# Identity products on TensorE in the first four chunks of a selective scan

## The chip, the core and the metric

The kernel runs on one core of one Trainium2 chip. The metric is the device time of one execution in microseconds (us). In what follows PE is TensorE, DVE is VectorE, ACT is ScalarE, POOL is GpSimd and SP is the engine that issues most transfers.

## What is computed

The input is 2 sequences of 1024 tokens with 256 features. Four blocks follow one another, each with a residual sum and a layer norm ahead of it: a selective state-space scan, a mixture of 8 experts (top 2, with a capacity), linear attention with 16 heads, and a gated feed-forward layer. The scan is the part that matters here:

```python
A = -jnp.exp(A_log)                                  # 256 features x 64 states
def step(h, inp):
    dt, b, xt, c = inp
    dA = jnp.exp(dt[:, :, None] * A)
    h = dA * h + dt[:, :, None] * b[:, None, :] * xt[:, :, None]
    y = jnp.einsum('bdn,bn->bd', h, c)
    return (h, y)
```

Each of the 2 x 1024 tokens thus updates a state of 256 x 64 numbers and reads it out once.

## The kernel before

`prepare` norms and projects the tokens and writes the factors of the scan to HBM as sums of bf16 parts. `selective_scan` then goes over 32 chunks of 64 tokens (16 chunks a sequence), and each chunk over 8 groups of 16 pairs of features. There are 256 groups, numbered gi; c = gi // 8 is the chunk and j = gi % 8 the group in it. `rest` does the experts, the attention and the feed-forward layer.

For a group the engines do this, in the names and lines of the profile:

- PE computes the exponents of the decays into two PSUM banks, `bank_a` (L911, 16 products of 64 columns in bf16, function `decays`). There is one pair of these banks, so `decays(gi)` waits until ACT has read those of the group before (semaphore `exp`, L904).
- ACT turns them into decays (L1045, two exponentials a group) and, in all chunks but the first of a sequence, puts the carried state of the chunk before into the input (L1055, `hand_on`), which POOL has computed (L1315, L1321). In ACT's order the hand-on of group gi stands behind both exponentials of group gi + 1.
- PE computes the inputs of the recurrence (L930, 16 products in bf16) into one of two double banks, `bank_in`. It waits there for the scan two groups back (L925).
- DVE runs the recurrence over the group (L1160, one instruction of 128 x 1024).
- From group 10 on, PE reads the states of the chunk before out (L944, function `y`), four float32 products of 32 rows by 512 columns at a time, behind the inputs of every even group.

`scan_schedule` writes one list, and every engine goes through it in this order. PE's `stream(gi)` issues `decays(gi + 1)` and then the inputs of group gi. The first product on a new chunk's tokens is L970, which waits for the transfer of the chunk (`tokens_ld`). From group 34 on, every odd group is preceded by `stay_awake`: two bf16 products of 128 x 512 on a constant matrix (L898), written over a bank that `decays` fills directly afterwards. Nobody reads their result. The constant, `tri`, is loaded and cast only at group 32. Ahead of that PE has no such products.

A float32 product stands as two records in the profile, a float32 transpose as one.

Of the kernel before, what the change touches and what calls it, by code (L numbers as in the profile page):

```python
# [7 lines left out]
P = 128  # L8
# [46 lines left out]
class Kit:  # L55
# [11 lines left out]
    def sem(self, name):  # L67
        if name not in self.named:
            self.named[name] = self.ctx.enter_context(self.nc.semaphore("s_" + name))
        return self.named[name]  # L70
# [47 lines left out]
CPB = SEQ // T  # L118
G = 16
GROUPS = P // G  # L120
# [660 lines left out]
def selective_scan(k, a, s):  # L781
    pe, act, dve, pool, sp, sem = k.pe, k.act, k.dve, k.pool, k.sp, k.sem
    ident, eps, slots = s["ident"], s["eps"], s["slots"]
    with ExitStack() as ctx:
# [28 lines left out]
        bank_a = [k.banks[0], k.banks[1]]  # L813
# [79 lines left out]
        def on_pe():  # L893
            def stay_awake(bank):

                pe.wait_ge(sem("tri"), 1)
                for _ in range(2):
                    pe.q.matmul(bank, tri[:, 1, :], tri[:, 1, :].unsqueeze(1).broadcast_to([P, 4, P]), start=True, stop=True)  # L898

            def decays(gi):  # L900
                c, j = divmod(gi, GROUPS)
                pe.wait_ge(sem(f"rows_ld{c % 2}"), ROWS_LD * (c // 2 + 1))
                if gi:
                    pe.wait_ge(sem("exp"), 2 * gi)  # L904
                if j % 2 and gi > GROUPS * CPB // 4 + 1:
                    stay_awake(bank_a[1])
                for i in range(8):
                    for half in range(2):
                        g, q = divmod(first_d(j, half) + i, RCH)
                        strip = slice(32 * g, 32 * (g + 1))  # L910
                        ins = pe.q.matmul(bank_a[half][:, i * T:(i + 1) * T], s["astat"][strip, RCH * g + q, :],  # L911
                                          rows[strip, c % 2, q, :], start=True, stop=True)
                ins.then_inc(sem("prod"), 1)

            def stream(gi):
                c, j = divmod(gi, GROUPS)
                if gi == 0:
                    pe.wait_ge(sem("astat_ld"), 16 * ROWG * DH * 3)
                    wait_prepared(k, pe)
                    decays(0)  # L920
                if gi + 1 < TOTAL:
                    decays(gi + 1)
                pe.wait_ge(sem(f"tokens_ld{c % 2}"), TOKENS_LD * (c // 2 + 1))
                if gi >= 2:
                    pe.wait_ge(sem("scan"), gi - 1)  # L925
                for half in range(2):
                    d = slice(first_d(j, half), first_d(j, half) + 8)
                    for b in range(BLKS):
                        to = per_d(bank_in[gi % 2])[:, 8 * half:8 * half + 8, S * b:S * (b + 1)]
                        ins = pe.q.matmul(to.rearrange("p d (s e) -> p s d e", e=2), bstat[0:ROWS, c % 2, b, :],  # L930
                                          xdiag[0:ROWS, c % 2, b, :, d, :], start=True, stop=True)
                ins.then_inc(sem("inputs"), 1)
# [27 lines left out]
            for kind, *x in schedule:  # L960
# [59 lines left out]
                elif kind == "rank":  # L1020
# [9 lines left out]
                    for i in range(n - 1):  # L1030
# [3 lines left out]
                                start=False, stop=True).then_inc(sem("r_rank"), 1)  # L1034
# [308 lines left out]
        on_sp()  # L1343
        on_act()
        on_pe()
        on_dve()
        on_pool()
# [655 lines left out]
```

## Time and profile before

| | |
|---|---|
| three timed executions | 1318.41, 1318.73, 1331.76 us; median 1318.73 |
| profiled execution | 1323.35 us, span 1321.8 us |
| mean granted TensorE clock | 0.913 |
| PE busy | 1116.7 us, 84% of the span |
| DVE busy | 842.4 us, 64% |
| ACT busy | 502.7 us, 38% |
| DVE, the recurrence (L1160) | 256 instructions, 565.3 us busy, from 100.9 to 694 us of the span |
| PE, read-out (L944) | 1024 records, 155.0 us |
| PE, `stay_awake` (L898) | 222 records, 69.0 us |

The span falls into `prepare` (to about 96 us), the scan (to about 694 us), the routing and scatter of the last tokens (to 738 us), the experts (to about 1025 us), and attention and feed-forward. The clock column of the profile gives the mean granted clock of a stretch as a share of 2.4 GHz: 0.50 is 1.2 GHz throughout, 1.00 is 2.4 GHz throughout.

### The profile page before, as it was taken

The numbers are of one execution on the slowest core, as the hardware profiler recorded it, in microseconds if no ns is written. First come the engines' busy times: TensorE is split into PE (matmuls) and PEld (weight loads), VectorE is DVE, ScalarE is ACT, GpSimd is POOL, SyncE is SP. The second block draws the span as 40 slices with busy tenths as digits, with TensorE's granted clock in tenths as the row PEclk, the third lists the DMA queues.
The fourth block names the chain that finished last, engine by engine and source line by source line (L and its number), as shares of the span: only waits on it lengthen the run. The fifth ranks groups of instructions, "written<-read, shape, count | busy, mean of one in ns | idle before, by whom it ended". The sixth has DMA issues, their size and how long they took to land.

```text
span 1321.8 us, 29499 instructions
## 1 busy us (share of the span) xinstructions
PE 1116.7 (84%) x11952; PEld 705.4 (53%) x11952; DVE 842.4 (64%) x1006; ACT 502.7 (38%) x1245; POOL 306.9 (23%) x930
## 2 busy tenths in 40 slices
PE   3637888889888888889884799999999488999998
PEld 2425444445444454444442578888887244475565
DVE  5858999999999999999993111121111577742211
ACT  2865555566655665566551111111111110122110
POOL 9741222222233222522242011111111100000000
PEclk8765789989999898998996799999999798999999
DMA  3797345543222222322223822222200400000000
GB/s 106 235 283 217 76 99 128 132 115 84 55 64 70 56 60 48 85 57 50 52 70 143 299 95 102 100 100 99 79 17 12 131 0 0 0 9 8 16 16 16
DMA packets 171687, 112.02 MB, mean 85 GB/s; under 512 B 93637, under 2 KB 162248, under 8 KB 169248
## 3 DMA queue, kind: packets, MB, share of 16 engines
q1 hardware_dynamic: 163120, 88.69, 24.2%
q0 software_dynamic: 8000, 20.87, 4.8%
q8 instruction: 94, 1.54, 0.5%
q10 hardware_dynamic: 432, 0.59, 0.2%
q14 instruction: 41, 0.34, 0.1%
HBM read 63.18 MB, written 45.90 MB: 83 GB/s over the span
## 4 chain that ended last, share of the span: by engine, by line
PE 48%; DVE 27%; issue 13%; ACT 4%; DMA 3%; SPq 2%; POOL 1%; DVEq 0%; POOLq 0%; ACTq 0%
DVE h L1160 19%; PE psum L1410 11%; PE psum L1422 10%; PE psum L1894 8%; PE psum L1905 4%; PE psum L944 3%; DVE den L1724 2%; PE psum L1850 2%; PE psum L930 2%; ACT decay L1045 2%; PE psum L911 2%; DMA b_parts_d<-b_parts 1%; PE psum L1842 1%; PE psum L1881 1%; PE psum L898 1%
## 5 line engine op out<-in xcount | busy, mean ns | idle before, releaser
L1160 DVE TENSOR_TENSOR_SCAN h<-decay,psum 128x1024 f32<-128x1024 f32 x256 | 565.3, 2266 | 16.9 <-ACT psum L1055 9.9
L1045 ACT ACTIVATE decay<-psum 128x512 f32<-128x512 f32 x512 | 279.3, 600 | 201.9 <-PE psum L911 197.1
L930 PE MATMUL psum<-xdiag,bstat 96*128 96x64 bf16 x4096 | 178.5, 201 | 50.2 <-DVE h L1160 47.2
L930 PEld LDWEIGHTS psum<-xdiag,bstat 96*128 96x128 bf16 x4096 | 146.8, 102 | 76.4 <-DVE h L1160 68.1
L911 PEld LDWEIGHTS psum<-rows,shared 32*128 32x128 bf16 x4096 | 79.8, 97 | 186.9 <-issue 120.3
L944 PE MATMUL psum<-h,cstat 128*32 128x512 f32 x1024 | 155.0, 683 | 1.6 <-DVE h L1160 1.6
L1410 PE MATMUL psum<-xdt,shared 128*128 128x320 f32 x512 | 141.7, 438 | 0.7 <-ACT xdt L1469 0.7
L1422 PE MATMUL psum<-shared,hid 128*128 128x256 f32 x640 | 139.5, 379 | 0.6 <-ACT hid L1463 0.6
L1315 POOL TENSOR_TENSOR carry<-decay,h 128x16 f32<-128x16 f32 x240 | 57.9, 241 | 343.9 <-ACT decay L1045 343.6
L1422 PEld LDWEIGHTS psum<-shared,hid 128*128 128x128 f32 x640 | 121.0, 190 | 17.2 <-issue 1.1
L911 PE MATMUL psum<-rows,shared 32*128 32x64 bf16 x4096 | 111.4, 196 | 15.4 <-ACT decay L1045 7.5
L1410 PEld LDWEIGHTS psum<-xdt,shared 128*128 128x128 f32 x512 | 98.7, 193 | 41.7 <-issue 2.8
L1894 PE MATMUL psum<-xt,wgu 128*128 128x512 f32 x256 | 112.8, 600 | 2.5 <-DVE at L1729 2.5
L1497 DVE TENSOR_SCALAR hid<-psum 128x320 f32<-128x320 f32 x64 | 31.4, 491 | 112.9 <-PE psum L1410 112.9
L1532 POOL DMA_INDIRECT picked_d<-eo,to x40 | 39.0, 975 | 259.5 <-ACT eo L1466 134.2
L898 PE MATMUL psum<-r_tri 128*128 128x512 bf16 x222 | 69.0, 393 | 28.8 <-ACT decay L1045 28.2
L1500 DVE TENSOR_SCALAR eo<-psum,gate 128x256 f32<-128x256 f32 x20 | 9.7, 484 | 116.9 <-PE psum L1422 111.2
L1894 PEld LDWEIGHTS psum<-xt,wgu 128*128 128x128 f32 x256 | 49.1, 192 | 64.2 <-issue 59.4
L1747 DVE TENSOR_TENSOR shared<-psum,sil 128x512 f32<-128x512 f32 x32 | 22.0, 691 | 81.5 <-PE psum L1894 81.5
L1463 ACT ACTIVATE hid<-psum 128x320 f32<-128x320 f32 x64 | 28.0, 437 | 119.1 <-PE psum L1410 119.1
L1818 ACT ACTIVATE sil<-psum 128x512 f32<-128x512 f32 x32 | 19.1, 597 | 131.2 <-PE psum L1894 127.1
L1321 POOL TENSOR_TENSOR carry<-carry,u 128x16 f32<-128x16 f32 x240 | 52.9, 221 | 24.0 <-ACT u L1083 3.6
(194 smaller groups left out, 1103.0 us busy)
## 6 DMA issues: line engine op xcount, KB each, us to landing
shared<-in_w SPq DMA_DIRECT2D x16, 1024.0 KB, 4.8
xdiag<-x_parts_d SPq DMA_DIRECT2D x256, 48.0 KB
x_parts_d<-x_parts POOLq DMA_DIRECT2D x46, 256.0 KB, 8.0
parts_d<-dt_parts SPq DMA_DIRECT2D x24, 256.0 KB, 8.5
rows<-parts_d SPq DMA_DIRECT2D x128, 48.0 KB
disp_d<-zero SPq DMA_DIRECT2D x4, 1305.0 KB, 8.5
xd<-disp_d SPq DMA_DIRECT2D x8, 652.5 KB, 6.3
picked_d<-zero SPq DMA_DIRECT2D x4, 1024.0 KB, 5.2
```

What stands on the lines that cost most here:

```text
L898: pe.q.matmul(bank, tri[:, 1, :], tri[:, 1, :].unsqueeze(1).broadcast_to([P, 4, P]), start=True, stop=True)
L911: ins = pe.q.matmul(bank_a[half][:, i * T:(i + 1) * T], s["astat"][strip, RCH * g + q, :], rows[strip, c % 2, q, :], start=True, stop=True)
L930: ins = pe.q.matmul(to.rearrange("p d (s e) -> p s d e", e=2), bstat[0:ROWS, c % 2, b, :], xdiag[0:ROWS, c % 2, b, :, d, :], start=True, s ...
L944: ins = pe.q.matmul(bank_y[32 * q:32 * q + 32, :].rearrange("p (s d e) -> p s d e", s=2, e=4), s["cstat"][:, tok // 4, :], h[:, first:last ...
L1045: act.q.activation(decay[:, gi % NB, 8 * half:8 * half + 8, :], per_d(bank_a[half]), ACT.Exp).then_inc(sem("exp"), 1)
L1160: dve.q.tensor_tensor_scan(out=h[:, half_slot(c, half), ch:ch + G, :].rearrange("p d t -> p (d t)"), data0=decay[:, gi % NB, :, :].rearran ...
L1315: pool.q.tensor_tensor(whole, first, h[:, half_slot(c - 1, half), ch:ch + G, T - 1], ALU.mult).then_inc(sem("carry_made"), 1)
L1321: pool.q.tensor_tensor(whole.rearrange("p (h i) -> p h i", h=2), whole.rearrange("p (h i) -> p h i", h=2), own, ALU.add).then_inc(sem("car ...
L1410: ins = pe.q.matmul(table.bank(key)[:, 0:half_cap], w1[:, e % 2, dh, f * P:(f + 1) * P], xdt[:, e % 2, dh, c * half_cap:(c + 1) * half_cap ...
L1422: ins = pe.q.matmul(table.bank(key)[:, 0:D], hid[:, e % 2, f, st * P:(st + 1) * P], w2[:, e % 2, f, :], start=f == 0, stop=f == FT - 1)
L1894: ins = pe.q.matmul(table.bank(key)[:, :], wgu[:, j, dh, f * P:(f + 1) * P], xt[:, u, dh, :], start=dh == 0, stop=dh == 1)
L1905: ins = pe.q.matmul(table.bank(key)[:, 0:D], gt[:, blk % 2, f, n * P:(n + 1) * P], wd[:, f, :], start=f == 0, stop=f == FT - 1)
```

## The change

A second helper, `wake`, issues one float32 product of the identity with itself over 256 columns, into the first half of the second bank of `bank_a`. `decays` calls it behind its wait for `exp` and ahead of its own products: for the groups 1 to 10 all, and for the odd groups from 11 to 33. These are 22 products. `ident` is there from the start of `prepare`. The result is overwritten by `decays` and is read by nobody. No wait is added, and nothing else of the program changes.

```diff
--- before.py
+++ after.py
@@ -897,11 +897,17 @@
                 for _ in range(2):
                     pe.q.matmul(bank, tri[:, 1, :], tri[:, 1, :].unsqueeze(1).broadcast_to([P, 4, P]), start=True, stop=True)
 
+            def wake(bank):
+
+                pe.q.matmul(bank[:, 0:2 * P], ident[:, :], ident[:, :].unsqueeze(1).broadcast_to([P, 2, P]), start=True, stop=True)
+
             def decays(gi):
                 c, j = divmod(gi, GROUPS)
                 pe.wait_ge(sem(f"rows_ld{c % 2}"), ROWS_LD * (c // 2 + 1))
                 if gi:
                     pe.wait_ge(sem("exp"), 2 * gi)
+                if gi and (j % 2 or gi <= GROUPS + 2) and gi <= GROUPS * CPB // 4 + 1:
+                    wake(bank_a[1])
                 if j % 2 and gi > GROUPS * CPB // 4 + 1:
                     stay_awake(bank_a[1])
                 for i in range(8):
```

Lines behind the helper move down by 6, so that L911 is L917 in the changed kernel, and so on. The new product is L902.

On PE, at the start of the scan, this stood before (L609 is the last of `prepare`; the two first groups' exponents follow it):

```order
L609 MATMUL psum<-ident,sp_r 128x128 x8
L911 MATMUL psum<-rows,shared 128x64 x32
L930 MATMUL psum<-xdiag,bstat 128x4x8x2 x16
L911 MATMUL psum<-rows,shared 128x64 x16
L930 MATMUL psum<-xdiag,bstat 128x4x8x2 x16
```

and this stands there now:

```order
L609 MATMUL psum<-ident,sp_r 128x128 x8
L917 MATMUL psum<-rows,shared 128x64 x16
L902 MATMUL psum<-ident 128x256
L917 MATMUL psum<-rows,shared 128x64 x16
L936 MATMUL psum<-xdiag,bstat 128x4x8x2 x16
L902 MATMUL psum<-ident 128x256
L917 MATMUL psum<-rows,shared 128x64 x16
L936 MATMUL psum<-xdiag,bstat 128x4x8x2 x16
```

The second group's exponents, and with them the first group's inputs, now stand behind an identity product.

On PE, where the second chunk begins, this stood before (L970 is the product that waits for the chunk's tokens, L944 the first read-out):

```order
L930 MATMUL psum<-xdiag,bstat 128x4x8x2 x16
L970 MATMUL psum<-xdiag,bstat 128x128
L911 MATMUL psum<-rows,shared 128x64 x16
L930 MATMUL psum<-xdiag,bstat 128x4x8x2 x16
L911 MATMUL psum<-rows,shared 128x64 x16
L930 MATMUL psum<-xdiag,bstat 128x4x8x2 x16
L911 MATMUL psum<-rows,shared 128x64 x16
L930 MATMUL psum<-xdiag,bstat 128x4x8x2 x16
L944 MATMUL psum<-h,cstat 32x512 x4
```

and this stands there now:

```order
L976 MATMUL psum<-xdiag,bstat 128x128
L902 MATMUL psum<-ident 128x256
L917 MATMUL psum<-rows,shared 128x64 x16
L936 MATMUL psum<-xdiag,bstat 128x4x8x2 x16
L902 MATMUL psum<-ident 128x256
L917 MATMUL psum<-rows,shared 128x64 x16
L936 MATMUL psum<-xdiag,bstat 128x4x8x2 x16
L902 MATMUL psum<-ident 128x256
L917 MATMUL psum<-rows,shared 128x64 x16
L936 MATMUL psum<-xdiag,bstat 128x4x8x2 x16
L950 MATMUL psum<-h,cstat 32x512 x4
```

The exponents of the chunk's second and third groups stand behind an identity product too; from there on only each second group's do, and these are the groups whose `decays` is followed by a read-out.

## Rows read from the trace of the kernel before

**Rows 1.** The page: granted clock in 40 slices of 33 us, in tenths.

```profile
PEclk8765789989999898998996799999999798999999
```

**Rows 2.** What DVE's recurrence waited for: us in total, times.

```profile
  ACT psum L1055: 9.9, 17
  POOL decay L1324: 5.5, 1
```

**Rows 3.** Timeline of DVE: start, us, instruction, count, in brackets the idle time ahead.

```profile
100.87 17.53 DVE L1160 TENSOR_TENSOR_SCAN h<-decay,psum 128x1024 f32<-128x1024 f32 x8 [5.47 <-POOL decay L1324]
119.70 6.64 DVE L1160 TENSOR_TENSOR_SCAN h<-decay,psum 128x1024 f32<-128x1024 f32 x3 [1.30 <-ACT psum L1055]
126.82 4.46 DVE L1160 TENSOR_TENSOR_SCAN h<-decay,psum 128x1024 f32<-128x1024 f32 x2 [0.48 <-ACT psum L1055]
131.98 4.46 DVE L1160 TENSOR_TENSOR_SCAN h<-decay,psum 128x1024 f32<-128x1024 f32 x2 [0.70 <-ACT psum L1055]
137.06 13.25 DVE L1160 TENSOR_TENSOR_SCAN h<-decay,psum 128x1024 f32<-128x1024 f32 x6 [0.61 <-ACT psum L1055]
150.83 8.82 DVE L1160 TENSOR_TENSOR_SCAN h<-decay,psum 128x1024 f32<-128x1024 f32 x4 [0.52 <-ACT psum L1055]
159.87 17.53 DVE L1160 TENSOR_TENSOR_SCAN h<-decay,psum 128x1024 f32<-128x1024 f32 x8 [0.23 <-ACT psum L1055]
178.20 2.29 DVE L1160 TENSOR_TENSOR_SCAN h<-decay,psum 128x1024 f32<-128x1024 f32 x1 [0.80 <-ACT psum L1055]
```

**Rows 4.** Busy time by stretch: PE, PEld, DVE, ACT, POOL, then clock, DMA share, GB/s.

```profile
98.00:115.00 17.00, 12.50 (x256) 10.61 (x256) 14.13 (x7) 9.12 (x18) 1.72 (x10) 0.50 0.84 247
118.00:135.00 17.00, 16.02 (x244) 9.62 (x238) 14.53 (x8) 9.53 (x30) 4.43 (x23) 0.50 0.75 198
135.00:142.00 7.00, 5.23 (x140) 3.51 (x137) 6.39 (x4) 5.14 (x16) 1.76 (x9) 0.96 0.47 80
180.00:190.00 10.00, 8.36 (x186) 4.48 (x179) 10.00 (x7) 5.42 (x16) 2.93 (x15) 1.00 0.56 160
```

**Rows 5.** Timeline of PE: two groups of chunk 0, and a read-out at half clock.

```profile
98.81 0.61 PE L911 MATMUL psum<-rows,shared 32*128 32x64 bf16 x16 [2.54 <-ACT decay L1045]
100.59 0.61 PE L911 MATMUL psum<-rows,shared 32*128 32x64 bf16 x16 [0.21 <-ACT decay L1045]
...
128.17 1.94 PE L944 MATMUL psum<-h,cstat 128*32 128x512 f32 x8
130.04 0.60 PE L911 MATMUL psum<-rows,shared 32*128 32x64 bf16 x16
```

**Rows 6.** Timeline of PE: the nearest products, at full clock and at half.

```profile
182.09 0.60 PE L898 MATMUL psum<-r_tri 128*128 128x512 bf16 x2 [0.61 <-ACT decay L1045]
182.62 0.41 PE L911 MATMUL psum<-rows,shared 32*128 32x64 bf16 x16
...
508.54 2.05 PE L955 MATMUL psum<-w_out,y_t 128*128 128x256 f32 x4
510.38 0.88 PE L898 MATMUL psum<-r_tri 128*128 128x512 bf16 x2
```

**Rows 7.** Timeline of all engines where the second chunk begins.

```profile
117.65 0.28 PE L970 MATMUL psum<-xdiag,bstat 12*128 12x128 bf16 x1 [2.50 <-DMA xdiag<-x_parts_d]
```

**Rows 8.** Timeline of PE in `prepare`.

```profile
35.51 1.09 PE L569 MATMUL psum<-ident,xa 128*128 128x128 f32 x4 [4.30 <-DVE xa L477]
39.34 1.40 PE L609 MATMUL psum<-ident,sp_r 128*128 128x128 f32 x8 [0.18 <-DVE sp_r L514]
40.58 1.88 PE L579 MATMUL psum<-xn_t,w_proj 128*128 128x512 f32 x4
```

**Rows 9.** Busy time by stretch around them, columns as in Rows 4.

```profile
36.00:38.00 2.00, 2.00 (x11) 2.00 (x10) 1.20 (x1) 1.43 (x2) 2.00 (x5) 0.50 0.21 14
40.00:42.00 2.00, 2.00 (x11) 1.28 (x10) 2.00 (x4) 1.64 (x3) 0.66 (x2) 1.00 0.10 30
```

**Rows 10.** Waits of DVE from 186 to 700 us: total, times, longest.

```profile
DVE h L1160 <- ACT psum L1055: 5.3, 10, 1.0
DVE h L1160 <- PE psum L930: 1.1, 2, 0.9
```

## The prediction, made before the changed kernel ran

> **What bounds the kernel now.** The change touches the scan's first 34 groups alone, so I ask which engine sets the pace there. I began with the page's clock line [rows 1]: the third to sixth slices, which hold the end of `prepare` and the first chunks of the scan, show 6, 5, 7 and 8 tenths, and only then does the clock stay near full. Next I asked what DVE's recurrence waited for [rows 2], because 256 instructions of 2.2 us each fill most of the 594 us of the scan: it waited 9.9 us for the hand-on of the carried state and 5.5 us for its very first group. DVE is thus the bound, and the change can win only time in which DVE stood idle. The timeline gives each gap [rows 3]. Chunk 0 runs without one, 8 recurrences in 17.53 us (2.19 us each). Chunk 1 begins 1.30 us late. Then come six gaps, 0.48 + 0.70 + 0.61 + 0.52 + 0.23 + 0.80 = 3.34 us. The recurrences of the groups behind 178.20 us are outside the change.
>
> The six gaps are PE's. From 118 to 135 us PE was busy for 16.02 of 17 us at clock 0.50, which is 1.2 GHz [rows 4], and two recurrences that DVE does in 4.46 us came every 131.98 - 126.82 = 5.16 us [rows 3]. At that clock a read-out takes 130.04 - 128.17 = 1.87 us [rows 5]. Where the clock is at its upper level, 2.4 GHz, and two `stay_awake` products stand ahead of every second group, PE has room: 8.36 us busy of 10 and DVE busy throughout [rows 4]. In that kernel part the products stand in the same place in each pair of groups as the new ones will.
>
> The gap of 1.30 us is not PE's clock but a transfer: L970 sat 2.50 us and started at 117.65 us when the chunk's tokens landed [rows 7]. DVE had ended chunk 0 at 118.40 us (100.87 + 17.53) and began chunk 1 at 119.70 us [rows 3], 2.05 us behind L970.
>
> **The cost of one identity product.** The trace has none. It is bounded from two sides by the nearest rows [rows 6]. Two bf16 products over 512 columns took 182.62 - 182.09 = 0.53 us at 2.4 GHz. Two float32 products over 256 columns took 510.38 - 508.54 = 1.84 us at 1.2 GHz, 0.92 us each, half of which is 0.46 us at 2.4 GHz. A float32 product over 256 columns is what is added, so it costs 0.5 us at 2.4 GHz and 0.95 us at 1.2 GHz; the bounds are 0.46 to 0.53 and 0.92 to 1.06 us. It stands behind PE's wait for ACT and ahead of `decays`, so it lengthens the loop in which `decays` waits for ACT's exponentials and ACT waits for `decays`.
>
> **Chunk 0, a loss.** The clock is 0.50 when the scan begins [rows 4]. The first recurrence waits for the inputs of group 0, which now stand behind one identity product: +0.95 us. The loop took 100.59 - 98.81 = 1.78 us a group [rows 5], hidden under DVE's 2.19 us. With the product it takes 2.73 us while the clock is low: the second recurrence is late by about 0.1 us (the first was ready half a microsecond early), each further one by 2.73 - 2.19 = 0.54 us. At 2.4 GHz the loop is below 1.78 + 0.5 - 0.2 us (0.61 us of `decays` shrinks to 0.41 [rows 5, 6]), some 2.1 us, and hidden. How soon the clock rises is not shown. It rose within 40.6 - 35.5 = 5 us of the start of nearly gapless full-size products in `prepare` [rows 8, 9]; chunk 0 had small products only, 12.50 us busy of 17, and it did not rise at all [rows 4]. So the ends are 5 us, two groups, and the whole chunk, eight. Full-size products now fill 0.95 of 2.73 us, so it will be later than 5 us; I take four groups, of which the recurrence pays 0.1 + 0.54, and part of one more: 0.8 us. Chunk 0 ends 0.95 + 0.8 = 1.75 us later, at 120.15 us. The ends are +1.05 and 0.95 + 0.1 + 6 x 0.54 = +4.3 us.
>
> **The step into chunk 1.** DVE had 1.30 us to spare here, and the transfer lands when it did. Behind L970 one more identity product stands ahead of the second group's exponents, and the hand-on of the first group stands behind these on ACT: 2.05 + 0.5 - 0.2 = 2.35 us behind 117.65 us is 120.0 us at 2.4 GHz, and 2.05 + 0.95 = 3.0 us, 120.65 us, at 1.2 GHz. DVE begins at the later of this and its own end of chunk 0, near 120.15 us: 0.45 us later than before. The ends are +0.3 us and 118.40 + 4.3 - 119.70 = +3.0 us.
>
> **The six gaps, a gain.** If the clock is at its upper level from there on, PE's work in a pair of groups is that of 180 to 190 us, where DVE had no gap [rows 4]. All 3.34 us go. If the clock falls as often as before, none goes and each product adds to a pair that is full already. I take the first, since the same place in the order with the same PE time held the clock at 1.00 there.
>
> **The sum.** +0.45 - 3.34 = -2.9 us against the profiled execution's 1323.35 us: 1320.5 us. Nothing between chunk 4 and the end of the scan has slack ahead of DVE, so the shift reaches the end. The three timed executions have their median 4.6 us below the profiled one, so the time to forecast is 1318.73 - 2.9 = 1315.8, rounded to **1316 us**. Its own range is 1312 to 1320: the ends of the first two terms, and the later gaps. For these are not constant. After 186 us DVE still lost 5.3 + 1.1 us [rows 10] in places where the clock fell for some microseconds in spite of `stay_awake`; where they fall hangs on how the scan lies in time, and a shift of some microseconds may take or add 3 us.
>
> **Rival one: the clock rises late** (slower than before). The mechanism is the loop through ACT. In chunk 0 the identity products lengthen it past DVE's pace from the second group on. If the clock is still low when chunk 1 begins, the step costs +3.0 us, the products of groups 9 and 10 another 2 x 0.95 on a PE without room, and one more pair 0.95 us; after that the clock is up, and 0.61 + 0.52 + 0.23 + 0.80 = 2.16 us of gaps go. Net +3.0 + 1.9 + 0.95 - 2.16 = +3.7 us: 1322.4 us. It decides where chunk 0 has more than about seven groups at 1.2 GHz. For it speaks that from 118 to 135 us PE was all but gaplessly busy and the clock stayed low [rows 4]; against it, that these were narrow products and the new ones are full-size.
>
> **Rival two: identity products don't raise the clock.** Then the step costs +3.0, groups 9 and 10 cost 1.9, and the twelve odd groups 11 to 33 between 8 x 0.95 (those in stretches that were at 1.2 GHz) and 12 x 0.95: together +12.5 to +16.3 us, in the middle 1333 us. Against it stand rows of `prepare`: from 35.51 to 40.58 us PE ran nothing but products with the identity (L569, L609) [rows 8], and the clock went from 0.50 to 1.00 [rows 9]. The Trainium skill, page "TensorE: Matmul & The Clock Gate", section "Part 4: PE-mode transpose", says that the upper clock level does not engage for transposes. By that rule the products of `prepare` would not have raised it, and identity products here might be no better; the trace disagrees. The new product is moreover a plain product and no transpose.
>
> **Rival three: nothing is left of it.** The gain is made, and the later clock drops, shifted by 3 us, take it back: 1318.7 us, give or take 2. For it speaks that the later gaps sum to 6.4 us, twice the gain [rows 10].
>
> **How the numbers follow.** Forecast 0.55, late rise 0.2, no rise 0.05, nothing left 0.2. The range reaches from the forecast's lower end over rival three to just above rival one, 1312 to 1324.5 us; outside are rival two and the tails. One per cent is 13.2 us, about what a measurement of this kernel can tell from no change. DVE's idle time ahead of all recurrences together, 9.9 + 5.5 us and little more, would have to vanish for a gain of that size: 0.01. Slower by as much only by rival two and not all of it: 0.04. The rest, 0.95, is within 1%.
>
> **What would show it.** In the profile after: the first recurrence about 1 us later; the clock at 1.00 within chunk 0, by about 110 us, and through 118 to 178 us; DVE without gaps in chunks 1 to 3 and about 0.5 us late at group 8; the recurrence of group 33 some 3 us earlier than 178.2 us; L902 at 0.5 us. A clock of 0.50 in 120 to 135 us would prove the forecast wrong, as would gaps of 1 us or more between pairs of recurrences there; a scan that is 3 us shorter with a total that is not would speak for rival three.

## The result, and the profile after

The changed kernel took 1327.63 us in the median of 19 runs (1321.08 to 1334.23), the kernel before 1322.74 us in as many (1315.98 to 1331.76). The ratio is 1.0037, 95% interval 1.0019 to 1.0055: 0.37% slower, some 4.9 us, where 2.9 us faster was forecast. The profiled execution took 1331.37 us, its span is 1329.9 us. Of the ten timed runs of the second measurement of the changed kernel, one took 5321.5 us and is not in its ratio below.

The page of the changed kernel gives the granted clock in 40 slices of 33 us. It answers to [rows 1]: the fourth slice is still at 5 tenths, the fifth at 8.

```profile
PEclk9865899998998898998996799999999798999999
```

What the recurrence waited for (us in total, times), as in [rows 2]. A new entry stands first: the inputs of the recurrence themselves, PE's products, now come late. Of its 13.4 us, 8.22 lie ahead of the first recurrence; before, that wait was 5.5 us under another name [rows 2].

```profile
  PE psum L936: 13.4, 10
  ACT psum L1061: 12.2, 20
```

The timeline of DVE in the changed kernel (start, us, instruction, count, in brackets the idle time ahead) answers to [rows 3].

```profile
101.07 4.46 DVE L1166 TENSOR_TENSOR_SCAN h<-decay,psum 128x1024 f32<-128x1024 f32 x2 [8.22 <-PE psum L936]
106.14 2.29 DVE L1166 TENSOR_TENSOR_SCAN h<-decay,psum 128x1024 f32<-128x1024 f32 x1 [0.61 <-PE psum L936]
109.08 2.29 DVE L1166 TENSOR_TENSOR_SCAN h<-decay,psum 128x1024 f32<-128x1024 f32 x1 [0.65 <-PE psum L936]
...
120.90 2.29 DVE L1166 TENSOR_TENSOR_SCAN h<-decay,psum 128x1024 f32<-128x1024 f32 x1 [0.71 <-PE psum L936]
124.10 2.29 DVE L1166 TENSOR_TENSOR_SCAN h<-decay,psum 128x1024 f32<-128x1024 f32 x1 [0.92 <-ACT psum L1061]
...
139.67 2.29 DVE L1166 TENSOR_TENSOR_SCAN h<-decay,psum 128x1024 f32<-128x1024 f32 x1 [1.09 <-ACT psum L1061]
...
145.55 41.66 DVE L1166 TENSOR_TENSOR_SCAN h<-decay,psum 128x1024 f32<-128x1024 f32 x19 [0.66 <-ACT psum L1061]
187.13 0.40 DVE L1190 TENSOR_TENSOR x1o<-psum,xres 128x256 f32<-128x256 f32 x1
```

In chunk 0 a recurrence now starts every 2.94 us (109.08 - 106.14) and not every 2.19. From group 15 at 145.55 us to group 33 there is no gap at all. PE's timeline shows the loop, and the price of one product at either clock.

```profile
109.19 1.22 PE L902 MATMUL psum<-ident 128*128 128x256 f32 x2 [0.21 <-ACT decay L1051]
110.34 0.61 PE L917 MATMUL psum<-rows,shared 32*128 32x64 bf16 x16
110.88 1.03 PE L936 MATMUL psum<-xdiag,bstat 96*128 96x64 bf16 x16
112.13 1.22 PE L902 MATMUL psum<-ident 128*128 128x256 f32 x2 [0.21 <-ACT decay L1051]
...
121.01 1.22 PE L902 MATMUL psum<-ident 128*128 128x256 f32 x2
122.16 0.61 PE L917 MATMUL psum<-rows,shared 32*128 32x64 bf16 x16
...
145.40 0.70 PE L902 MATMUL psum<-ident 128*128 128x256 f32 x2 [0.45 <-ACT decay L1051]
146.03 0.41 PE L917 MATMUL psum<-rows,shared 32*128 32x64 bf16 x16
```

A product holds the exponents back by 110.34 - 109.19 = 1.15 us at 1.2 GHz and by 146.03 - 145.40 = 0.63 us at 2.4 GHz; the loop is 112.13 - 109.19 = 2.94 us. The stretches (PE, PEld, DVE, ACT, POOL, clock, DMA share, GB/s) show when the clock rose; they answer to [rows 4].

```profile
98.00:115.00 17.00, 14.51 (x188) 9.97 (x186) 11.36 (x6) 6.50 (x12) 0.63 (x5) 0.50 0.75 217
118.00:135.00 17.00, 16.27 (x198) 10.00 (x199) 12.98 (x6) 7.16 (x23) 3.04 (x16) 0.50 0.73 170
135.00:142.00 7.00, 6.78 (x89) 4.04 (x89) 5.22 (x3) 3.01 (x8) 1.17 (x6) 0.50 0.01 2
142.00:149.00 7.00, 6.47 (x120) 3.25 (x117) 5.74 (x3) 3.92 (x14) 1.76 (x9) 0.89 0.26 41
149.00:160.00 11.00, 8.90 (x186) 5.40 (x190) 11.00 (x6) 6.35 (x17) 2.93 (x15) 1.00 0.25 70
```

It did not rise in chunk 0 at all, and only in chunk 1: 0.89 over the 7 us from 142 us puts the rise at about 143.5 us, 8 us later than before (0.96 over the 7 us from 135 us [rows 4], 135.5 us). The times of rise and fall below are read in the same way.

To compare many kernels I cut each profile at five points of DVE's timeline: the first recurrence, the end of group 7, the start of group 8, the start of group 15, and the end of group 33 (the first residual sum). From group 33 to the end of the last recurrence no kernel here is changed. In us:

| kernel | chunk 0 | step | 8 to 15 | 15 to 33 | sum | 33 to end |
|---|---|---|---|---|---|---|
| before | 17.53 | 1.30 | 17.36 | 43.35 | 79.54 | 513.8 |
| before, second profile | 17.53 | 1.25 | 16.64 | 43.03 | 78.45 | 513.5 |
| the change | 22.12 | 0.91 | 21.45 | 41.58 | 86.06 | 515.0 |
| the change, second profile | 22.55 | 0.91 | 17.37 | 41.43 | 82.26 | 511.1 |
| groups 1 to 10 only | 22.55 | 0.91 | 16.83 | 42.97 | 83.26 | 512.0 |
| odd groups 11 to 33 only | 17.53 | 0.92 | 16.82 | 41.44 | 76.71 | 511.0 |
| the same, again | 17.53 | 0.45 | 16.65 | 41.43 | 76.06 | 513.3 |
| odd groups 17 to 33 only | 17.45 | 0 | 16.61 | 41.40 | 75.46 | 511.1 |
| odd 11 to 33, bf16 | 17.53 | 0.20 | 16.63 | 41.40 | 75.76 | 509.5 |
| burst only | 17.45 | 0 | 16.64 | 43.33 | 77.42 | 519.7 |
| burst and the change | 22.13 | 0.91 | 17.97 | 41.43 | 82.44 | 511.1 |
| longer burst and the change | 19.98 | 0.91 | 17.97 | 41.44 | 80.30 | 509.7 |
| four products in groups 1 to 4 | 23.10 | 0.91 | 17.97 | 41.44 | 83.42 | 513.8 |
| the change, bf16 | 20.85 | 0.72 | 17.60 | 41.39 | 80.56 | 520.4 |
| the change, half size | 19.13 | 0.49 | 18.33 | 41.40 | 79.35 | 508.8 |

Behind the scan all spans agree, 626.1 to 628.5 us. The step aside, the first four columns follow the edits for the most part. Where chunk 0 has no products, the step hangs on when the chunk's tokens land, and differs between two profiles of one program (0.92 and 0.45 us). The last column differs by up to 11.6 us between profiles though no edit touches it. Its two highest values are from single executions 8 and 10 us above the median of their kernel (1331.15 against 1323.31 us for the bf16 change, 1328.71 against 1319.18 us for the burst). So one total tells little of an edit worth 3 us.

### The profile page after: what moved, and what is told of

Read it like the earlier page. It is cut to its first block, busy times and chain, and to the rows that moved or that the text cites. A ratio compares the mean times of both kernels' runs of the same rounds, so it can differ in the third digit from the quotient of the medians.

```text
span 1329.9 us, 29587 instructions
## 1 busy us (share of the span) xinstructions
PE 1132.8 (85%) x11996; PEld 713.5 (54%) x11996; DVE 843.9 (63%) x1006; ACT 502.2 (38%) x1245; POOL 307.2 (23%) x930
## 4 chain that ended last, share of the span: by engine, by line
PE 48%; DVE 28%; issue 13%; ACT 4%; SPq 3%; DMA 2%; POOL 1%; DVEq 0%; ACTq 0%; POOLq 0%
DVE h L1166 20%; PE psum L1416 11%; PE psum L1428 10%; PE psum L1900 8%; PE psum L1911 4%; PE psum L950 3%; DVE den L1730 2%; PE psum L1856 2%; PE psum L936 2%; PE psum L917 2%; ACT decay L1051 2%; PE psum L902 1%; PE psum L1848 1%; PE psum L1887 1%; SPq L199 1%
## 5 line engine op out<-in xcount | busy, mean ns | idle before, releaser
L1166 DVE TENSOR_TENSOR_SCAN h<-decay,psum 128x1024 f32<-128x1024 f32 x256 | 566.7, 2268 | 25.9 <-PE psum L936 13.4
L917 PEld LDWEIGHTS psum<-rows,shared 32*128 32x128 bf16 x4096 | 79.0, 97 | 182.6 <-issue 125.1
L917 PE MATMUL psum<-rows,shared 32*128 32x64 bf16 x4096 | 110.5, 195 | 5.2 <-DVE x_parts L540 4.7
L1824 ACT ACTIVATE sil<-psum 128x512 f32<-128x512 f32 x32 | 19.1, 597 | 131.2 <-PE psum L1900 127.1
```

The costliest lines, as they stand in the source:

```text
L1166: dve.q.tensor_tensor_scan(out=h[:, half_slot(c, half), ch:ch + G, :].rearrange("p d t -> p (d t)"), data0=decay[:, gi % NB, :, :].rearran ...
```

## The experiments

The diffs are against the changed kernel. `...` marks what is left out.

**Which products lose, which gain.**

```diff
-                if gi and (j % 2 or gi <= GROUPS + 2) and gi <= GROUPS * CPB // 4 + 1:
+                if gi and gi <= GROUPS + 2:
```

> Only the ten identity products of groups 1 to 10 are kept. The theory is that the loss lies in the groups before the clock rises, where a product costs 1.15 us and lengthens the loop between PE and ACT: then chunk 0 takes about 22 us against 17.5, chunk 1 begins some 4.4 us late, the products of groups 9 and 10 add about 1.3 us, and the kernel is 4.5 to 6.5 us slower than before, about 1327 to 1329 us on the scale of a median of 1322.7. The rival, that the odd products of groups 11 to 33 carry the loss, expects no more than 1 us of loss here. A second rival, that the clock rises in the second chunk sooner because of the early products, expects it at 1.00 before 135 us.

Measured: ratio 1.0034 (1.0012 to 1.0056). Chunk 0 took 22.55 us. The loss is here. Without the odd products two gaps stood between groups 15 and 33 again (42.97 us). The second rival's number came, the clock rose at 132.3 us and not before the first read-out, but by itself it decides nothing: in the kernel before it rose at 130.4 us in the second profile. More on this stands under "Only behind the rise".

```diff
-                if gi and (j % 2 or gi <= GROUPS + 2) and gi <= GROUPS * CPB // 4 + 1:
+                if j % 2 and GROUPS + 2 < gi <= GROUPS * CPB // 4 + 1:
```

> Only the twelve identity products of the odd groups 11 to 33 are kept. The theory expects chunk 0 as before (17.5 us), a loss of 1.1 us for each of the products of groups 11 and 13 and part of that for 15 while the clock is 0.50, and then a gain of about 1.6 us once it has risen and no longer falls: between 0 and 2 us slower than before. The rival that identity products cannot hold the clock expects the gaps near 151, 160 and 178 us still there, and 5 us or more of loss.

Measured: ratio 0.9974 (0.9949 to 1.0000), better than expected; the repeat below did not confirm it. DVE's timeline of this kernel:

```profile
99.81 17.53 DVE L1166 TENSOR_TENSOR_SCAN h<-decay,psum 128x1024 f32<-128x1024 f32 x8 [6.37 <-PE psum L936]
118.26 4.46 DVE L1166 TENSOR_TENSOR_SCAN h<-decay,psum 128x1024 f32<-128x1024 f32 x2 [0.92 <-ACT psum L1061]
123.11 2.29 DVE L1166 TENSOR_TENSOR_SCAN h<-decay,psum 128x1024 f32<-128x1024 f32 x1 [0.38 <-ACT psum L1061]
126.36 50.24 DVE L1166 TENSOR_TENSOR_SCAN h<-decay,psum 128x1024 f32<-128x1024 f32 x23 [0.96 <-ACT psum L1061]
```

Chunk 0 is whole again, and 23 recurrences follow without a gap, over the places of five of the six old ones; only the one ahead of group 11 stayed, with a smaller one ahead of group 10. The clock rose at 126.0 us and did not fall before 214 us. Identity products do hold the clock, once it is up and the read-outs run.

**Can identity products raise the clock?** Both kernels of this pair have a burst behind the preparation; the first has no product in the groups (the condition is `False`).

```diff
+            b = (table.of["tx", 3, 1][0] + 1) % 8
+            pe.wait_ge(table.evac[b], k.products[b])
+            for _ in range(6):
+                pe.q.matmul(k.banks[b][:, 0:2 * P], ident[:, :], ident[:, :].unsqueeze(1).broadcast_to([P, 2, P]), start=True, stop=True)
...
                     decays(0)
+                    for _ in range(2):
+                        wake(bank_z)
```

> No products in the groups at all; instead six identity products behind the last transposes of the preparation, where PE is idle for 5 to 7 us, and two more between the exponents of groups 0 and 1, where it waits for ACT. If identity products can raise the clock when they are dense, it is 1.00 when the scan begins; if what they lack is the type or the data, it stays at 0.50. The theory (dense enough, they can) expects 1.00 at about 95 us and a fall back to 0.50 within chunk 0, since the small products of a group do not hold it: the time is then that of before, within 1 us. If the clock should hold, the gaps of chunk 1 go and it is 2 to 4 us faster.

Measured: ratio 0.9982 (0.9960 to 1.0004). The clock by stretch:

```profile
90.00:92.00 2.00, 2.00 (x6) 1.62 (x5) 2.00 (x4) 2.00 (x3) 2.00 (x5) 0.50 0.99 194
94.00:96.00 2.00, 1.02 (x4) 0.57 (x4) 0.00 (x0) 1.93 (x3) 2.00 (x5) 1.00 1.02 373
98.00:100.00 2.00, 0.00 (x0) 0.00 (x0) 0.00 (x0) 0.03 (x1) 0.13 (x1) 0.95 1.03 385
100.00:102.00 2.00, 1.89 (x40) 1.72 (x41) 0.36 (x1) 0.27 (x1) 0.00 (x0) 0.50 1.02 357
```

Dense identity products raised it, so neither type nor data is in the way. The Trainium skill's rule that transposes do not engage the upper clock (page "TensorE: Matmul & The Clock Gate", section "Part 4: PE-mode transpose") cannot be carried over to plain products with the identity: these raised it. Then PE waited for the first tokens from 97 to 100 us, and the clock fell at 99.8 us, ahead of the first group's inputs.

> The dense products of the run before and all 22 of the change. If the change failed only because the clock was low when its products began, then with the clock up at about 95 us they hold it at 1.00 through chunks 0 to 3, each costs 0.63 us and is hidden, DVE has no gap from group 9 on, and the kernel is 3 to 4 us faster than before and 8 us faster than the change. If the wait of the products in the loop between PE and ACT costs time whatever the clock is, it is slower than before by 2 us or more. If the clock falls in chunk 0 in spite of the products, it is as slow as the change.

Measured: ratio 1.0054 (1.0024 to 1.0083). The clock fell in the same wait, at 98.8 us, and chunk 0 took 22.13 us. That looks like the third case of the expectation, but the clock was low before all but the first of the products in the groups, so this run does not show what they do at 2.4 GHz; the next one does.

**The same with the wait filled.**

```diff
+                for _ in range(5 if gi == 0 else 0):
+                    wake(bank_z)
                 pe.wait_ge(sem(f"tokens_ld{c % 2}"), TOKENS_LD * (c // 2 + 1))
```

> The burst, all 22 products of the change, and five more identity products ahead of the inputs of group 0, where PE waited 2 to 3 us for the first tokens and the clock fell in the last run. If the clock then enters the groups at 1.00, this shows what the products of the change do at 2.4 GHz. The theory: one product a group holds it, each costs 0.63 us, the loop of PE and ACT stays below DVE's 2.2 us, chunk 0 takes 17.5 us again and DVE has no gap from group 9 on; 2 to 4 us faster than before. The rival that the place in the loop costs time at any clock expects gaps of 0.3 us or more in chunk 0 at clock 1.00. A second rival, that one product a group is too little to hold it, expects 0.50 within chunk 0 and the time of the change.

Measured, from only four timed runs: ratio 1.0061 (1.0037 to 1.0084). DVE's timeline, and then the clock by stretch:

```profile
102.22 11.09 DVE L1174 TENSOR_TENSOR_SCAN h<-decay,psum 128x1024 f32<-128x1024 f32 x5 [9.24 <-PE psum L944]
113.97 2.29 DVE L1174 TENSOR_TENSOR_SCAN h<-decay,psum 128x1024 f32<-128x1024 f32 x1 [0.65 <-PE psum L944]
```

```profile
98.00:100.00 2.00, 2.00 (x6) 1.55 (x6) 0.00 (x0) 0.35 (x1) 0.12 (x1) 0.50 1.01 378
102.00:104.00 2.00, 1.39 (x35) 1.05 (x34) 1.77 (x1) 1.08 (x2) 0.13 (x1) 1.00 1.03 340
104.00:106.00 2.00, 1.39 (x35) 0.89 (x34) 2.00 (x2) 1.09 (x2) 0.02 (x1) 1.00 1.01 299
108.00:110.00 2.00, 1.80 (x21) 1.07 (x22) 2.00 (x2) 0.15 (x2) 0.13 (x1) 0.50 0.53 78
```

The clock fell at 97.7 us all the same, and rose again at 101.1 us under the five new products, just ahead of the first recurrence. PE had waited 1.47 us for ACT up to 96.19 us and was busy from then on, so the wait for the tokens is not shown to be what brought the clock down in the two runs before. At 1.00, with one product a group, five recurrences ran without a gap: the place in the loop is harmless at 2.4 GHz, and the first rival falls. But PE was busy for 1.39 of 2 us there, and the clock fell near 108 us: the second rival holds. One product a group does not keep it up in chunk 0.

**More products.**

```diff
-                    wake(bank_a[1])
+                    for _ in range(4 if gi <= 4 else 1):
+                        wake(bank_a[1])
```

> As the change, but four identity products instead of one in each of groups 1 to 4. If one product a group was too thin to raise the clock, it rises here within the first two groups, after 5 to 8 us of dense products; the sixteen products then cost some 9 us at first, and from group 5 on the recurrences follow each other every 2.2 us at clock 1.00. Chunk 0 then ends no later than 3 us behind the change's. If identity products in the groups do not raise it whatever their number, each group of 1 to 4 takes 2.94 + 3 x 1.1 = 6.2 us, the kernel is 13 us slower than the change, and the clock is 0.50 until about 155 us.

Measured: ratio 1.0042 (1.0023 to 1.0060). PE's timeline, first in group 2 with its four products (eight records), then behind the four groups that have four, and the clock:

```profile
101.09 1.99 PE L902 MATMUL psum<-ident 128*128 128x256 f32 x8 [0.60 <-ACT decay L1052]
103.02 0.41 PE L918 MATMUL psum<-rows,shared 32*128 32x64 bf16 x16
...
111.63 0.70 PE L902 MATMUL psum<-ident 128*128 128x256 f32 x2 [0.60 <-ACT decay L1052]
113.84 0.70 PE L902 MATMUL psum<-ident 128*128 128x256 f32 x2 [0.61 <-ACT decay L1052]
116.06 1.12 PE L902 MATMUL psum<-ident 128*128 128x256 f32 x2 [0.61 <-ACT decay L1052]
```

```profile
98.00:100.00 2.00, 2.00 (x26) 1.43 (x25) 0.00 (x0) 0.04 (x1) 0.00 (x0) 0.72 1.04 393
102.00:104.00 2.00, 2.00 (x38) 1.42 (x36) 1.27 (x1) 0.53 (x2) 0.00 (x0) 1.00 1.03 350
114.00:116.00 2.00, 1.46 (x34) 0.95 (x34) 2.00 (x2) 1.08 (x2) 0.00 (x0) 1.00 0.81 260
116.00:118.00 2.00, 1.94 (x25) 1.21 (x26) 1.85 (x1) 0.25 (x2) 0.13 (x1) 0.55 1.03 337
```

Four products in a row raised the clock at about 99 us and held it for four groups; two groups with one product each followed at 1.00, and in the third it fell. So what was missing in chunk 0 is the number of products, and not their kind: with one a group the clock did not rise there or stay up, but the loop was already lengthened. Chunk 0 was within 3 us of the change's, as expected; the recurrences did not follow each other without a gap to its end, since the clock had fallen again at 116.2 us.

**Type and data.** The matrix of ones is filled by POOL ahead of everything else.

```diff
...
-                pe.q.matmul(bank[:, 0:2 * P], ident[:, :], ident[:, :].unsqueeze(1).broadcast_to([P, 2, P]), start=True, stop=True)
+                pe.wait_ge(sem("ones"), 1)
+                for _ in range(2):
+                    pe.q.matmul(bank, s["ones"][:, :], s["ones"][:, :].unsqueeze(1).broadcast_to([P, 4, P]), start=True, stop=True)
```

> All 22 products of the change, but as two bf16 products of 512 columns on a matrix of ones, which is the form and the data of those that hold the clock later on. If it was the type or the data, the clock rises in chunk 0 and there is no gap from about group 4 on: 2 us faster than before. If not, the clock stays at 0.50 as in the change, and only the price differs: 0.97 us instead of 1.15, so the groups 2 to 15 have 0.18 us less each and the kernel is about 2 us faster than the change and 2.5 us slower than before.

Measured: ratio 1.0037 (1.0017 to 1.0057). From PE's timeline:

```profile
105.27 1.03 PE L905 MATMUL psum<-ones_bf 128*128 128x512 bf16 x2 [0.21 <-ACT decay L1054]
106.23 0.61 PE L920 MATMUL psum<-rows,shared 32*128 32x64 bf16 x16
...
108.02 1.03 PE L905 MATMUL psum<-ones_bf 128*128 128x512 bf16 x2 [0.21 <-ACT decay L1054]
```

The pair costs 106.23 - 105.27 = 0.96 us, the loop is 2.75 us, the clock stays at 0.50 until about 130 us. Type and data are out; only the price differs, and chunk 0 with it (20.85 us against 22.12). In the total the 2 us that this should give against the change are not seen: its ratio is that of the change, and an interval of 0.2% either way is 2.6 us. Behind group 33 this profile took 520.4 us, the most of all.

**Size.**

```diff
-                pe.q.matmul(bank[:, 0:2 * P], ident[:, :], ident[:, :].unsqueeze(1).broadcast_to([P, 2, P]), start=True, stop=True)
+                pe.q.matmul(bank[:, 0:P], ident[:, :], ident[:, :], start=True, stop=True)
```

> All 22 products of the change at half the size, 128 columns. If the loss of chunk 0 is the product's length in the loop of PE and ACT, 1.79 + about 0.6 = 2.4 us a group against DVE's 2.19, chunk 0 takes 17.5 + 6 x 0.2 = 18.8 us, and the whole loss of chunk 0 is 1 to 1.5 us instead of 4.5. If something else that comes with a product costs the time (a switch between float32 and bf16, a drained pipeline), the gaps stay near 0.65 us. The clock stays at 0.50 in chunk 0 either way; after it the kernel is between 1 us faster and 3 us slower than before.

Measured: ratio 1.0015 (0.9989 to 1.0041). From DVE's timeline:

```profile
110.53 2.29 DVE L1166 TENSOR_TENSOR_SCAN h<-decay,psum 128x1024 f32<-128x1024 f32 x1 [0.23 <-PE psum L936]
113.04 2.29 DVE L1166 TENSOR_TENSOR_SCAN h<-decay,psum 128x1024 f32<-128x1024 f32 x1 [0.23 <-PE psum L936]
```

A recurrence every 2.51 us: 1.78 + 0.73 for the smaller product. Three sizes of the loop, 2.94, 2.75 and 2.51 us, gave chunk 0 in 22.12, 20.85 and 19.13 us. Against 17.53 us that is 4.6, 3.3 and 1.6 us, or about six times what the loop exceeds 2.19 us by, less a little in the last: the loss is the product's length in the loop. The total cannot tell this kernel from the one before. At half the size the products still held the clock: after its rise at 133.0 us it did not fall before 293 us.

**Only behind the rise.**

```diff
-                if gi and (j % 2 or gi <= GROUPS + 2) and gi <= GROUPS * CPB // 4 + 1:
+                if j % 2 and 2 * GROUPS < gi <= GROUPS * CPB // 4 + 1:
```

> Products only in the odd groups 17 to 33, behind the first rise of the clock. If what pays is only holding the clock, the gaps of groups 11, 13 and 15 stay (1.8 us), those near groups 21, 25 and 33 go (1.55 us): 1.6 us faster than before. If the products of groups 11 to 15 also made the clock rise sooner, this is 0.5 to 1 us slower than the run with the odd groups 11 to 33, though it has none of their products at 1.2 GHz.

Measured: ratio 0.9994 (0.9979 to 1.0008). Groups 15 to 33 took 41.40 us, as with all products; groups 8 to 15 took 16.61 us, as without. In DVE's time the products of groups 11 to 15 neither helped nor hurt. The gain expected, 1.6 us or 0.12%, lies inside the interval and is shown by the profile alone.

They did bring the rise of the clock forward. Counted from the start of group 8, it came 11.0 to 15.8 us later in the four profiles without a product in groups 9 to 11 (the kernel before twice, the burst alone, and this one). It came 6.3 to 8.7 us later in nine of the ten profiles that have full-size ones there (one float32 or two bf16), and 19.4 us later in the tenth, the first profile of the change; with products of half the size it was 12.1 us. In the runs with the odd products the earlier rise gave DVE back about what they cost it at 1.2 GHz (groups 8 to 15 in 16.82, 16.65 and 16.63 us).

**The version with the lowest ratio, twice more.** The edit of the odd groups 11 to 33 once more, and the same in bf16.

> The run with identity products in the odd groups 11 to 33 alone, again, since its interval of 0.9949 to 1.0000 just touched no change. The theory (no product before the first read-out) expects chunk 0 without gaps, the clock at 1.00 from about 126 us to the end of chunk 3, and a ratio of 0.997 to 0.999. If the earlier one was chance, the ratio is 1.000 or above.

Measured: ratio 1.0005 (0.9986 to 1.0023). The stretches repeat (76.06 us against 76.71), the ratio of 0.9974 does not: by the rule of the expectation it was chance.

> The same odd groups 11 to 33, with two bf16 products of 512 columns on ones in place of the identity product. While the clock is at 1.2 GHz a pair costs 0.97 us and not 1.15, at 2.4 GHz 0.54 and not 0.63. The theory expects the gaps of groups 11 and 13 to be 0.1 to 0.2 us shorter each and otherwise the same trace: a ratio as in the run beside it, within 0.1%. If data and type matter for holding the clock, gaps come back between 130 and 178 us.

Measured: ratio 1.0017 (0.9990 to 1.0045), the stretch 75.76 us. The gap ahead of group 10 was 0.20 us against 0.38 (the product of group 11 stands ahead of the inputs of group 10), that of group 11 unchanged. This version beats the change in the scan by 6 us and more, and by the profiles its stretch is 2.7 to 3.8 us shorter than before; 1.1 us of that is the step, which lies ahead of its first product and is not its doing. A gain in the total was not shown.

**Both kernels again.**

> The kernel before, once more. Over twelve profiles the part of the scan behind group 33, which no edit touched, took between 508.8 and 520.4 us; the first part took 79.5 us before. If the first part is set by the program and the second varies by itself, this profile shows 78 to 80 us in the first part, with the gaps of DVE in groups 11, 13 and 15 again, and anything between 508 and 521 us in the second. If the first part varies as much as the second, the +6.7 us read between the two first profiles says little.

Measured: ratio of the kernel before to itself 0.9994 (0.9975 to 1.0012), the stretch 78.45 us against 79.54. The gaps ahead of groups 11 and 13 were there again, that of group 15 was not: the clock rose at 130.4 us, and not at 135.5.

> The changed kernel, once more. Chunk 0 should take 22.1 us again, groups 15 to 33 41.4 to 41.6. Chunk 1 is the open term: 21.45 us in its first profile, where the clock rose behind the third read-out, and 17.97 us where the same products were there and it rose behind the first (the run with the burst and all products). If the time of the rise is chance, this profile may show either; the first part then takes 82.4 or 86.1 us. The median of the timed runs should be 4 to 5 us above that of before, which lies nearer to the first.

Measured: ratio 1.0043 (1.0020 to 1.0065), so the loss repeats. DVE's timeline where the clock rose, and the clock:

```profile
130.81 2.29 DVE L1166 TENSOR_TENSOR_SCAN h<-decay,psum 128x1024 f32<-128x1024 f32 x1 [0.78 <-ACT psum L1061]
133.46 50.24 DVE L1166 TENSOR_TENSOR_SCAN h<-decay,psum 128x1024 f32<-128x1024 f32 x23 [0.36 <-ACT psum L1061]
```

```profile
122.00:128.00 6.00, 5.58 (x69) 3.78 (x70) 4.43 (x3) 2.73 (x11) 1.22 (x7) 0.50 0.80 161
128.00:134.00 6.00, 5.39 (x80) 2.80 (x81) 4.87 (x3) 3.10 (x11) 1.40 (x8) 0.73 0.98 151
134.00:140.00 6.00, 5.39 (x117) 3.01 (x118) 6.00 (x3) 3.49 (x9) 1.48 (x9) 1.00 0.14 34
```

Here it rose in the first read-out, at about 131.2 us, and groups 8 to 15 took 17.37 us, against 17.36 and 16.64 us in the two profiles of before. The 4.1 us that the first profile lost there are thus chance, those of chunk 0 are not.

## Why the prediction was wrong

**The step that failed is the one on chunk 0**: "I take four groups". The clock rises in none of the eight. (The prediction had named its own sign: a clock of 0.50 in 120 to 135 us, which the stretches show.) I had taken the rise in `prepare` [rows 8, 9] as a bound, though PE ran full-size products there nearly without a gap, and in chunk 0 they fill less than half of the loop. The experiments show that one product a group neither raises the clock there nor, if it is up, holds it; four in a row do both. The end that I had named for this case, +4.3 us, looks nearly right, but partly by luck: 0.95 us of it is the late start, and the 3.34 us that remain for chunk 0 itself stand against 22.12 - 17.53 = +4.6 us in the first profile and +5.0 in the second.

**The price at 1.2 GHz was low.** I took 0.95 us from a float32 product and a bound of 1.06; it is 1.15 us. At 2.4 GHz it is 0.63 us, not 0.5. The row behind the estimate was a pair of float32 products with another full-size product behind it [rows 6]; the new one stands alone among small ones. The starts of the single records show the difference. At 1.2 GHz they follow each other by 0.43 us within such a series, but 0.57 to 0.59 us pass from the first to the second, and 0.56 us from the last to the small product behind it. The pair of [rows 6] is 0.57 + 3 x 0.43 = 1.85 us, the new product 0.59 + 0.56 = 1.15 us. The run with four in a row agrees: they took 103.02 - 101.09 = 1.93 us at 2.4 GHz, and not 4 x 0.63. The wait for ACT ahead of the product is not the reason, since the one at 121.01 us, which waits for nothing, holds the next work back by 122.16 - 121.01 = 1.15 us too. The bf16 pair in the same place costs 0.96 us, less than the 1.06 worked out from its row. The error is 0.2 us a group, 1.2 us in chunk 0.

**The first recurrence** was to start 0.95 us later. It started at 101.07 and 101.35 us against 100.87 and 99.78. In the first profile PE waited for the chunk's tokens until 99.54 us, and the product was hidden in that wait. In the second it was paid: from PE's first exponents to the first recurrence took 101.35 - 94.99 = 6.36 us, against 5.21 us in both profiles of before, 1.15 us more.

**The step into chunk 1** was a maximum of two times, and both came out beyond their worst ends. I had let PE reach L976 when the transfer landed, at 117.65 us; behind the longer loop it came there only at 120.73 us, with no transfer to wait for. DVE ended chunk 0 at 123.19 us and then still waited 0.91 us. Chunk 1 began 4.4 us later than before, where +3.0 was the worst end.

**The six gaps**: those behind group 15 went, 43.35 to 41.58 us, 1.8 us. This part of the forecast was right, in mechanism and size, and it is the same in every kernel that has the odd products (41.39 to 41.58). Those ahead of groups 11, 13 and 15, 1.79 us, did not go in the first profile, since the clock was low there; in the second only 0.36 us ahead of group 11 was left of them. But both have new gaps of 0.65 and 0.78 us ahead of groups 9 and 10.

**The sum by terms**, from the two profiles of each kernel: chunk 0 +4.8 us, the step -0.4, groups 8 to 15 +2.4 (0 to +4.8), groups 15 to 33 -1.7, together +5.2 us. Left out are the time of the first recurrence (+0.9) and the part behind group 33 (-0.6), which differ as much between two profiles of one kernel. The timed runs say +4.9 us.

**The rivals.** Rival one, the late rise, is what happened: slower, by the loop through ACT. It gave +3.7 us; with 1.15 us for the product its step and its two products in groups 9 and 10 would have given some 2 us more. I gave it 0.2 for the reason that the new products are full-size, and had the row that spoke for it in hand: PE all but gaplessly busy at 0.50 from 118 to 135 us. Rival two, identity products cannot raise the clock, fell with the burst. Rival three, nothing left, needs the gain to be made first and then lost again. It was not made: up to group 33 the changed kernel lost 6.5 us in the first profiles and 3.8 in the second.

**The base.** I started from a median of three runs, 1318.73 us; over 19 it is 1322.74 us. With +4.9 us on the first base the time would have been 1323.6 us, inside the range, which held the rivals one and three. The missing 4 us are the scatter of this kernel from one set of runs to the next (its medians in the later sets were 1319.0 to 1321.3 us), but the sign was wrong by the mechanism.

## What to carry to other kernels

A product that is to wake or hold TensorE's clock costs most exactly while it is needed: price it at the lower clock, in the place where it stands, and ask which loop between engines it lengthens. Add such products only where the engine that sets the pace has gaps (chunk 0 had none to win), and where PE has work like the read-outs beside them. Even there, what was shown is 1.4 to 2 us fewer gaps in the profiles, and no gain in the total. Split a long kernel at points that no edit moves before judging an edit of some microseconds.

## What the runs showed of the hardware

The clock fell in both kernels with a burst in which PE then waited 2 to 3 us for a transfer, and also in the one where that wait was filled (at 97.7 us). In chunk 0 it fell with a full-size product of 0.63 us in every 2.2 us, and stayed low with one of 1.15 us in every 2.94 us. In chunks 1 to 3 it held at 1.00 with the same product in every second group beside a read-out of 1.0 us. The read-outs alone did not hold it either: in the kernel before and with the burst alone it fell several times between 140 and 176 us. When the clock rises in chunk 1 differs from one execution to the next of the same program: 131.2 and 143.5 us in two profiles of the changed kernel, 130.4 and 135.5 us in two of the kernel before. A float32 product with the identity over 256 columns costs 0.63 us at 2.4 GHz where it stands alone among small ones, and four in a row cost 1.93 us, so about 0.43 us for each further one.
